# Attention's constants made ahead of batch 0's rows, and the feed-forward weights rounded in nine blocks of columns

## The chip, the cores and the metric

The kernel runs on one core of a Trainium2 chip. The metric is the device time of one launch in microseconds. The core's engines work side by side and meet at semaphores only: TensorE (PE in the profile: matmuls), the vector engine (DVE), ScalarE (ACT), GpSimd (POOL) and SyncE (SP, which here only issues DMAs). Each takes its instructions in the order in which the program wrote them for it.

## What is computed

A "macaron" block over x of shape (8, 512, 256): half a feed-forward layer, an attention layer, half a feed-forward layer again, each on a layer norm of its input.

```python
x = x + 0.5 * ffn(layernorm(x))
x = x + attn(layernorm(x))
x = x + 0.5 * ffn(layernorm(x))

def ffn(x):                      # gate_w, up_w: (256, 768), down_w: (768, 256)
    gate = silu(quantized_matmul(x, gate_w, gate_scale))
    up = quantized_matmul(x, up_w, up_scale)
    return quantized_matmul(gate * up, down_w, down_scale)

def quantized_matmul(x, w, scale):
    return (x @ w.astype(float8_e4m3fn).astype(float32)) * scale
```

Attention is a gated delta rule with 16 heads of 128 channels, its sequence cut into chunks of 128 rows; the kernel solves each chunk's triangular system by a blocked inverse of six levels. For that it needs constants: an identity in f32 and f16, a few masks, and for each level a mask (`masks`) and a copy of the identity's right halves (`y16`).

## The kernel before

Three programs run one behind the other: `ffn_phase(first=True)`, `attention_phase` and `ffn_phase(first=False)`. Each ends with a barrier of all engines. The change touches the first only, which takes up to about 235 us of the span.

**Start of the first phase.** SyncE issues the loads: batch 0 of x, `gate_w`, batch 1, `up_w`, `down_w`, small things, then the other batches and the first four parts of the attention's weights. The DVE computes the statistics of batch 0 (`stats(0, 0)`), GpSimd the root and shift of the norm (`root(0, 0)`), ScalarE applies them (`normed(0, 0)`), TensorE transposes, ScalarE writes the high half in f16 (`high`) and the DVE the low half (`low(0, 0)`). Meanwhile the DVE rounds the three weights to the values of float8 e4m3, in `wq16`: for each weight six instructions over 128 x 1536 columns (lines 521 to 528), each waiting for the one before. It counts in `s_wd`. Between the first and the second weight stand `low(0, 0)` and `stats(0, 1)`. Then come four small instructions on the weights of the decays (the fourth raises `s_wd` to 4), and `hidden(0, 0)`.

**Turns.** Batch b has 512 rows and six blocks m of 128 hidden columns. For each block TensorE makes `gate(b, m)` and `up(b, m)` (four matmuls over 512 columns each), ScalarE `silu(b, m)`, the DVE `hidden(b, m)` (the product), ScalarE `hidden_high(b, m)`, GpSimd `low(b, m)` (the low half, L332) and TensorE `down(b, m)`. There are three buffers for the hidden block, so `hidden(b, m)` waits for `low` of three blocks ago, over batches too: `need(dve, g_hl, q - HB + 1)` with q = 6b + m and HB = 3. After block 5 the DVE scales (`added`, L434) and GpSimd adds to the rows (`added`, L342). Then the norm for attention of that batch runs in the next turn: `stats(1, b - 1)`, `root(1, b - 1)`, `normed(1, b - 1)`, transposes, `high(1)`, `low(1)`; and its decays (`decay_products`, `decays`, `logistic`, `cumulative`, `strengths`), which are stored as rows.

The order of each engine within a turn is written out by hand in `turn1(b)`. For GpSimd it is `low(b,0)`, `root(1,b-1)`, `low(b,1)`, `low(b,2)`, `low(b,3)`, `root(0,b+2)`, `low(b,4)`, `low(b,5)`, `added(b)`. Between two turns it makes constants: `attention_constants()` after turn 0, and `level_constants(li)`, li = b - 1, after turns 1 to 6. Every instruction of these waits for the one before (`chain`).

For the DVE it is `hidden(b,1)`, `stats(1,b-1)`, `hidden(b,2)`, `part_low(b,0)`, `hidden(b,3)`, `logistic(b-2)`, `stats(0,b+2)`, `hidden(b,4)`, `cumulative(b-2)`, `strengths(b-2)`, `low(1,b-1)`, `hidden(b,5)`, `part_low(b,1)`, `low(0,b+1)`, `added(b)`, `part_low(b,2)`, `hidden(b+1,0)`.

**Parts.** From turn 1 on three of the 20 parts of attention's weights are split in a turn, `part_high` on ScalarE and `part_low` (L473) on the DVE. The first five stay in SBUF; from the sixth on SyncE stores them, and `part_high` waits until its slot of two has been stored. ScalarE's order in a turn ends with `part_high(b+1,1)`, `silu(b+1,2)`, `hidden_high(b+1,1)`, `silu(b+1,3)`, `hidden_high(b+1,2)`, `decays(b-1)`, `normed(1,b)`, and the next begins with `silu(b,4)`.

Of the kernel before, what the change touches and what calls it, by code (L numbers as in the profile page):

```python
# [9 lines left out]
I32 = mybir.dt.int32  # L10
# [5 lines left out]
FF = 768  # L16
# [44 lines left out]
def ffn_phase(nc, first, x_in, y_out, stream, z16, kit, scratch, w):  # L61

    with ExitStack() as ctx:  # L63
# [36 lines left out]
        if first:  # L100
            wraw = sb("wraw", [P, 3 * KT * FF]); wexp = sb("wexp", [P, KT * FF])
# [4 lines left out]
            heads0 = sb("heads0", [NH, NC, CX]); blocks = sb("blocks", [P, P])  # L106
            raw = sb("raw", [P, RAW, PART]); pairs = sb("pairs", [P, 2, 2, PART], F16)
# [52 lines left out]
        def _(sp):  # L160
# [60 lines left out]
            if first:  # L221
# [7 lines left out]
                for x in range(RAW):  # L229
                    load_part(x)  # L230
                sp.wait_ge(s_wd, 4)
                sp.dma_start(w_saved, wq16[:, :]).then_inc(s_save, 16)
# [20 lines left out]
        def _(pool):  # L253
# [42 lines left out]
            def level_constants(li):  # L296

                if not 0 <= li < NL:
                    return
                mb, y16 = LEVELS[li], kit["y16"]  # L300
                nb = P // (2 * mb)

                blk = blocks[:, :].rearrange("p (b two m) -> p b two m", two=2, m=mb)[:, :, 0, :]
                chain(nc.gpsimd.memset(blocks[:, :], 0.0))
                chain(nc.gpsimd.memset(blk, -1.0))
                fill(blk, 0.0, ALU.is_ge, -mb, [[-2 * mb, nb], [0, mb]], 1)
                fill(blk, 0.0, ALU.is_ge, 2 * mb - 1, [[2 * mb, nb], [0, mb]], -1)
                fill(blocks[:, :], -1.0, ALU.not_equal, 0, [[-1, P]], 1)
                chain(nc.gpsimd.tensor_copy(kit["masks"][:, li].rearrange("p (b m) -> p b m", m=mb), blk))
                for u in range(U):  # L310
                    chain(nc.gpsimd.tensor_copy(halves(y16[:, li, u], mb, 1), halves(kit["ident"][:, :], mb, 1)))

# [65 lines left out]
        @block.vector  # L378
        def _(dve):
# [88 lines left out]
            def part_low(b, k):  # L468
                x = part_of(b, k)
                if x is None:  # L470
# [4 lines left out]
                    .then_inc(d_part, 1)  # L475

            def attention_scales():

                dve.wait_ge(s_prm, 16 * 8)
                nc.vector.tensor_scalar(prm[:, :, :, 0:TAPS], prm[:, :, :, 0:TAPS], 1.0 / WS, None, ALU.mult)  # L480
                nc.vector.tensor_scalar(lnwn[:, :], lnwn[:, :], -1.0, None, ALU.mult)

            def turn1(b):
                hidden(b, 1)
                stats(1, b - 1)
                hidden(b, 2)
                part_low(b, 0)
                hidden(b, 3)
# [24 lines left out]
            if first:  # L513
                stats(0, 0)
                for i in range(3):
                    r, q = wraw[:, i * KT * FF:(i + 1) * KT * FF], wq16[:, i * KT * FF:(i + 1) * KT * FF]
                    e = wexp[:, :]
                    dve.wait_ge(s_w[i], 16)


                    chain(nc.vector.tensor_scalar(e.bitcast(I32), r.bitcast(I32), 0x7F800000, None, ALU.bitwise_and))
                    chain(nc.vector.tensor_scalar(e, e, 2.0 ** -6, 1.5 * 2.0 ** 20, ALU.max, ALU.mult))
                    chain(nc.vector.tensor_tensor(r, r, e, ALU.add))
                    chain(nc.vector.tensor_tensor(r, r, e, ALU.subtract))


                    chain(nc.vector.tensor_scalar(e, r, 1.125 * 2.0 ** 119, 0.0, ALU.mult, ALU.mult))
                    nc.vector.tensor_tensor(q, r, e, ALU.add).then_inc(s_wd, 1)
                    dve.wait_ge(s_wd, i + 1)
                    if i == 0:  # L530
                        low(0, 0)
                        stats(0, 1)
                dve.wait_ge(s_small, 16 * 7)
# [9 lines left out]
            if first:  # L543
                hidden(0, 0)
                for b in range(0, B + 2):
                    turn1(b)
                    if b == 5:
                        attention_scales()
            else:
                for b in range(-3, B + 1):  # L550
                    turn2(b)

        @block.scalar
        def _(act):
# [95 lines left out]
            if first:  # L650
                normed(0, 0)
                high(0, 0)
                normed(0, 1)
            act.wait_ge(s_small, 16 * (7 if first else 3))
            if first:
                act.wait_ge(s_const, 8)
            if first:
# [11 lines left out]
        def _(pe):  # L669
# [20 lines left out]
            def gate(b, m):  # L690
                if not 0 <= b < B:
                    return
                q = MT * b + m
                if m == 0:
                    if b == 0:
                        pe.wait_ge(*((s_wd, 1) if first else (s_w[0], 16)))
                    pe.wait_ge(a_zh[0], KT * (b + 1))
                    pe.wait_ge(d_zl[0], KT * (b + 1))
# [3 lines left out]
            def up(b, m):  # L702
                if not 0 <= b < B:
                    return
                if m == 0 and b == 0:
                    pe.wait_ge(*((s_wd, 2) if first else (s_w[1], 16)))
                need(pe, a_sg, MT * b + m)
# [11 lines left out]
            def down(b, m):  # L719
# [3 lines left out]
                q = MT * b + m  # L723
                pe.wait_ge(g_hl, q + 1)
                if m == 0:
                    if b == 0:
                        pe.wait_ge(*((s_wd, 4) if first else (s_w[2], 16)))
                    need(pe, d_y, KT * b)
# [974 lines left out]
```

## Time and profile before

| | us |
|---|---|
| median of 3 runs (2473.37 to 2475.38) | 2474.54 |
| the profiled execution, whole | 2475.66 |
| its span in the profile | 2473.9 |
| busy TensorE | 2355.2 (95%) |
| busy DVE | 2017.3 (82%) |
| busy ScalarE | 1813.7 (73%) |
| busy GpSimd | 1824.8 (74%) |

The profile is of one execution. Times in its timeline are microseconds from the span's start. A row gives the start, the time taken, the engine, the line, the operation, the tiles (out<-in, the program's names with buffer numbers left out) and the shape; `x4` means that four in a row were merged, and the time is then of all four. In brackets stands how long the engine sat idle before and what ended that; "issue" is time in which it waited for nothing that the profile shows.

### The profile page before, as it was taken

Reading aid. Unit: us, or ns where it says so; the run is one execution under the profiler, and the core shown is the slowest. Engines: PE = TensorE matmul, PEld = TensorE weight load, DVE = VectorE, ACT = ScalarE, POOL = GpSimd, SP = SyncE. Lnnn points to the kernel's source line nnn. Section 1 sums busy time; section 2 is a strip of 40 time slices with the busy share of each in tenths; the row PEclk is TensorE's granted clock in tenths of the full one; section 3 lists DMA queues with packets and bytes.
Section 4 is the critical chain, followed back from the end, with each engine's and each line's share of the span. In section 5 each row is a group of like instructions: output and inputs, shape, how many; then the busy total and the mean of one; then the engine's idle time right before and its main releaser. Section 6 shows DMA issues by size and latency. Waiting matters only on the chain. (4 is left out here: it accounts for less than half of the span.)

```text
span 2473.9 us, 64148 instructions
## 1 busy us (share of the span) xinstructions
PE 2355.2 (95%) x24496; PEld 1825.3 (74%) x24496; DVE 2017.3 (82%) x4246; ACT 1813.7 (73%) x3567; POOL 1824.8 (74%) x1977
## 2 busy tenths in 40 slices
PE   4897899999999999999999999999999999998598
PEld 2553588888888888888888888888888878877365
DVE  7775888888888888888888888888888888886353
ACT  3673677777777777777777777777777777776364
POOL 4783577777777777777777877777777787777365
PEclk9998999999999999999999999999999999999699
DMA  6241011111121111111211111112211111111001
GB/s 165 91 144 43 27 32 32 30 27 30 31 57 49 31 32 31 32 32 32 52 52 30 32 32 32 32 31 49 54 30 29 31 32 32 32 32 23 22 32 38
DMA packets 72833, 103.59 MB, mean 42 GB/s; under 512 B 21456, under 2 KB 33744, under 8 KB 72400
## 3 DMA queue, kind: packets, MB, share of 16 engines
q1 hardware_dynamic: 72528, 99.48, 15.9%
q8 instruction: 197, 3.23, 0.5%
q14 instruction: 108, 0.88, 0.1%
HBM read 85.69 MB, written 13.77 MB: 40 GB/s over the span
## 5 line engine op out<-in xcount | busy, mean ns | idle before, releaser
L1598 PE MATMUL a_bank<-k_z,k_kqv 128*128 128x512 f16 x2304 | 598.9, 380 | 9.8 <-DVE a_qb L1173 3.8
L1287 ACT ACTIVATE a_inv<-a_bank 128x512 f16<-128x512 f32 x640 | 383.3, 599 | 207.0 <-PE a_bank L1447 191.2
L1104 DVE TENSOR_TENSOR k_y<-a_bank,k_masks 128x256 f16<-128x256 f32 x768 | 318.8, 415 | 126.0 <-PE a_bank L1433 122.0
L941 POOL TENSOR_TENSOR k_diag<-k_ident,k_bcol 128x512 f32<-128x512 f32 x128 | 132.9, 1038 | 228.7 <-DVE a_prod L1080 213.7
L1598 PEld LDWEIGHTS a_bank<-k_z,k_kqv 128*128 128x128 f16 x2304 | 198.1, 98 | 139.7 <-DVE a_kb L1173 5.9
L1173 DVE SCALAR_TENSOR_TENSOR a_kb<-a_bank,k_prm,a_kb 128x511 f32<-128x511 f32 (+2 forms) x384 | 283.1, 737 | 14.9 <-ACT a_kb L1231 14.4
L1173 DVE SCALAR_TENSOR_TENSOR a_vb<-a_bank,k_prm,a_vb 128x511 f32<-128x511 f32 (+2 forms) x384 | 283.9, 739 | 0.1
L1173 DVE SCALAR_TENSOR_TENSOR a_qb<-a_bank,k_prm,a_qb 128x511 f32<-128x511 f32 (+2 forms) x384 | 282.8, 737 | 0.4
L1447 PE MATMUL a_bank<-a_inv,k_y 128*128 128x64 f16 x3072 | 271.4, 192 | 1.0 <-DVE k_y L1104 1.0
L1445 PE MATMUL a_bank<-k_y,a_inv 128*128 128x64 f16 x2560 | 236.0, 193 | 4.8 <-DVE k_y L1104 2.2
L1433 PEld LDWEIGHTS a_bank<-a_inv,a_am 128*128 128x128 f16 x3072 | 168.1, 98 | 94.4 <-ACT a_inv L1287 5.6
L1447 PEld LDWEIGHTS a_bank<-a_inv,k_y 128*128 128x128 f16 x3072 | 207.1, 98 | 34.2 <-DVE k_y L1104 1.3
L1445 PEld LDWEIGHTS a_bank<-k_y,a_inv 128*128 128x128 f16 x2560 | 197.1, 98 | 43.7 <-DVE k_y L1104 17.7
L953 POOL TENSOR_TENSOR a_am<-a_at,k_ident 128x512 f16<-128x512 f32 x128 | 163.7, 1279 | 82.0 <-DVE a_at L1089 82.0
L1029 POOL TENSOR_SCALAR a_gb<-a_gb 128x512 f32<-128x512 f32 x128 | 219.7, 1716 | 1.2 <-ACT a_gb L1251 1.2
L1433 PE MATMUL a_bank<-a_inv,a_am 128*128 128x64 f16 x3072 | 215.6, 193 | 4.3 <-ACT a_inv L1287 4.0
L1598 PE MATMUL a_bank<-k_z,k_gate 128*128 128x512 f16 x768 | 200.8, 379 | 0.2 <-DVE a_vb L1173 0.2
L1578 PE MATMUL a_bank<-k_wo,a_oh 128*128 128x256 f16 x1024 | 191.2, 275 | 9.6 <-POOL a_ol L1045 9.3
L1312 ACT ACTIVATE a_on<-a_bank,a_shift,a_rstd 128x128 f32<-128x128 f32 x512 | 191.7, 463 | 6.6 <-POOL a_shift L1021 6.5
L1540 PE MATMUL a_bank<-a_wv,a_mix 128*128 128x128 f32 x1024 | 185.6, 278 | 0.7 <-DVE a_wv L1123 0.7
L1080 DVE TENSOR_TENSOR_SCAN a_prod<-a_decay,k_diag 128x516 f32<-128x516 f32 x128 | 182.2, 1424 | 1.2 <-ACT a_kdec L1262 1.2
L1038 POOL TENSOR_TENSOR a_oa<-a_oa,a_gb 128x512 f32<-128x512 f32 x128 | 163.0, 1274 | 22.4 <-ACT a_oa L1321 21.7
(152 smaller groups left out, 6696.7 us busy)
## 6 DMA issues: line engine op xcount, KB each, us to landing
a_decay<-decay_rows SPq DMA_DIRECT2D x128, 258.0 KB, 3.8
a_cum<-cumulative_rows SPq DMA_DIRECT2D x96, 258.0 KB, 3.6
weight_pairs<-f_pairs SPq DMA_DIRECT2D x15, 512.0 KB, 2.9
k_kqv<-weight_pairs SPq DMA_DIRECT2D x9, 512.0 KB, 4.7
stream<-in_L_attn_x SPq DMA_DIRECT2D x8, 512.0 KB, 6.8
out<-stream SPq DMA_DIRECT2D x8, 512.0 KB, 2.9
f_raw<-in_L_attn_Wk SPq DMA_DIRECT2D x4, 512.0 KB, 4.8
f_raw<-in_L_attn_Wq SPq DMA_DIRECT2D x4, 512.0 KB, 5.0
```

Source lines behind the costliest of these rows:

```text
L1029: nc.gpsimd.tensor_scalar(gb[:, n % 2, j], gb[:, n % 2, j], 1.0, None, ALU.add).then_inc(m["pool_one"], 1)
L1080: nc.vector.tensor_tensor_scan(prod[:, :], decay[:, :], diag[:, :, :].rearrange("p u x -> p (u x)"), 0.0, ALU.mult, ALU.add).then_inc(m["d ...
L1104: nc.vector.tensor_tensor(even(y16[:, j], mb), bank[LEV[par]][:, 0:U * C // 2].rearrange("p (u b m) -> p u b m", u=U, m=mb), masks[:, j].r ...
L1173: nc.vector.scalar_tensor_tensor(out=dst[:, d:S], in0=bank[PJ[j % 2]][:, 0:S - d], scalar=prm[:, i, U * (n // B) + j, TAPS - 1 - d:TAPS - ...
L1287: nc.scalar.activation(both, bank[LEV[par]][:, :].rearrange("p (two b m) -> p two b m", two=2, m=mb), ACT.Copy).then_inc(m[f"act_lev{par}" ...
L1312: ins = nc.scalar.activation(on[:, u], bank[OUT][:, u * D:(u + 1) * D], ACT.Identity, bias=shift[:, u:u + 1], scale=rstd[:, u:u + 1])
L1433: mm = pe.matmul(at_half(LEV[par], 0, u), am16[:, par, u], halves(t16[par][:, u], mb, 0), start=True, stop=True)
L1445: pe.matmul(at_half(LEV[par], 0, u), tt16[par][:, u], halves(y16[:, j, u], mb, 0), start=True, stop=True)
L1447: mm = pe.matmul(at_half(LEV[par], half, u), y16[:, j, u], halves(tt16[par][:, u], mb, 1), start=True, stop=True)
L1540: mm = pe.matmul(units(OUT)[:, u], mix[:, t % 2, u], wv[:, u], start=not c, stop=True)
L1578: mm = pe.matmul(bank[SUM][:, 0:H], o[:, u], wo16[:, group % WO_SLOTS, wh, u], start=(u == 0 and wh == 0 and o is oh), stop=(u == U - 1 an ...
L1598: mm = pe.matmul(bank[PJ[j % 2]][:, :], wt, z16[:, zh, k, cols], start=(x == 0), stop=(x == 5))
```

## The change

Four things change, all in `ffn_phase(first=True)`.

1. The rounding goes by `quantise(i, x)`: a third of weight i, which is two of its six blocks of 128 hidden columns, so that each of the six instructions works on 128 x 512 columns. `wexp` is a third as large. `s_wd` now counts nine pieces, and ten with the small weights.
2. The DVE's order at the start becomes: (0,0), (1,0), (0,1), `low(0,0)`, (1,1), `hidden(0,0)`, (0,2), `hidden(0,1)`, `stats(0,1)`, (1,2), `hidden(0,2)`, (2,0), `hidden(0,3)`, (2,1), (2,2), the small weights, then turn 0 without its first `hidden`. On ScalarE `normed(0,1)` moves from ahead of `silu(0,0)` to behind `silu(0,3)`. TensorE waits in batch 0 for the piece that it needs, and `decay_products(0)` for `s_wd` = 10.
3. GpSimd makes all constants ahead of turn 0: `root(0,0)`, `attention_constants()`, `level_constants(0)`, `root(0,1)`, `level_constants(1..5)`, `turn1(0)`, and nothing between the turns.
4. `level_constants` builds its mask in place in f16, by a memset and three fills over 64 columns, in place of two memsets, three fills and a cast by way of `blocks`; its four copies read the identity in f16.

```diff
+ROUNDED = ((1, 3, 5), (2, 4, 6), (7, 8, 9))
...
-                sp.wait_ge(s_wd, 4)
+                sp.wait_ge(s_wd, 9)
                 sp.dma_start(w_saved, wq16[:, :]).then_inc(s_save, 16)
...
+                mask = kit["masks"][:, li].rearrange("p (b m) -> p b m", m=mb)
+                chain(nc.gpsimd.memset(mask, -1.0))
+                fill(mask, 0.0, ALU.is_ge, -mb, [[-2 * mb, nb], [0, mb]], 1)
+                fill(mask, 0.0, ALU.is_ge, 2 * mb - 1, [[2 * mb, nb], [0, mb]], -1)
+                fill(mask, -1.0, ALU.not_equal, 0, [[-2 * mb, nb], [-1, mb]], 1)
+                for u in range(U):
+                    chain(nc.gpsimd.tensor_copy(halves(kit["y16"][:, li, u], mb, 1),
+                                                halves(kit["ident16"][:, :], mb, 1)))
...
             if first:
                 root(0, 0)
+                attention_constants()
+                level_constants(0)
                 root(0, 1)
+                for li in range(1, NL):
+                    level_constants(li)
                 for b in range(0, B + 2):
                     turn1(b)
-                    if b == 0:
-                        attention_constants()
-                    level_constants(b - 1)
...
+            def quantise(i, x):
+
+                if x == 0:
+                    dve.wait_ge(s_w[i], 16)
+                r, q = third(wraw, i, x), third(wq16, i, x)
+                e = wexp[:, :].rearrange("p (k n) -> p k n", n=r.shape[2])
...
+                chain(nc.vector.tensor_scalar(e.bitcast(I32), r.bitcast(I32), 0x7F800000, None, ALU.bitwise_and))
+                chain(nc.vector.tensor_scalar(e, e, 2.0 ** -6, 1.5 * 2.0 ** 20, ALU.max, ALU.mult))
+                chain(nc.vector.tensor_tensor(r, r, e, ALU.add))
+                chain(nc.vector.tensor_tensor(r, r, e, ALU.subtract))
...
+                chain(nc.vector.tensor_scalar(e, r, 1.125 * 2.0 ** 119, 0.0, ALU.mult, ALU.mult))
+                nc.vector.tensor_tensor(q, r, e, ALU.add).then_inc(s_wd, 1)
+                dve.wait_ge(s_wd, ROUNDED[i][x])
...
                 stats(0, 0)
...
+                quantise(0, 0)
+                quantise(1, 0)
+                quantise(0, 1)
+                low(0, 0)
+                quantise(1, 1)
+                hidden(0, 0)
+                quantise(0, 2)
+                hidden(0, 1)
+                stats(0, 1)
+                quantise(1, 2)
+                hidden(0, 2)
+                quantise(2, 0)
+                hidden(0, 3)
+                quantise(2, 1)
+                quantise(2, 2)
```

## Rows read from the trace of the kernel before

**Rows 1.** Windows, 100 to 200 us: busy us by engine (instructions), granted clock, DMA share.
```profile
100.00:200.00 100.00, 90.84 (x540) 51.48 (x538) 77.10 (x144) 69.01 (x116) 80.16 (x113) 1.00 0.42 130
```

**Rows 2.** Timeline of the DVE, 7 to 46 us.
```profile
7.03 0.96 DVE L521 TENSOR_SCALAR f_wexp<-f_wraw 128x1536 int32<-128x1536 int32 x1 [0.15 <-DMA f_wraw<-in_L_ffn_gate_w]
...
9.03 1.76 DVE L523 TENSOR_TENSOR f_wraw<-f_wraw,f_wexp 128x1536 f32<-128x1536 f32 x1
...
37.01 1.41 DVE L423 SCALAR_TENSOR_TENSOR f_hid<-f_bank,f_us,f_sg 128x512 f32<-128x512 f32 x2
...
45.41 0.75 DVE L423 SCALAR_TENSOR_TENSOR f_hid<-f_bank,f_us,f_sg 128x512 f32<-128x512 f32 x1
```

**Rows 3.** Timeline of GpSimd, 9 to 62 us.
```profile
9.95 0.89 POOL L324 TENSOR_TENSOR f_shift<-f_nmean,f_rstd 128x4 f32<-128x4 f32 x1
...
55.58 0.20 POOL L282 MEMSET k_ident<- 128x128 f32 x1
...
57.23 2.66 POOL L286 MEMSET k_y<- 128x3072 f16 x1
...
61.67 1.15 POOL L332 TENSOR_TENSOR f_hl<-f_hid,f_hh 128x512 f16<-128x512 f32 x1
```

**Rows 4.** Groups by line and form, 0 to 225 us: xcount | busy us, mean ns | idle before.
```profile
L542 DVE TENSOR_SCALAR f_hds<-f_hds 128x256 f32<-128x256 f32 x1 | 0.3, 289 | 0.0
...
L537 DVE TENSOR_TENSOR f_wabl<-f_wab,f_wabh 128x64 f16<-128x64 f32 x1 | 0.2, 226 | 0.0
```

**Rows 5.** SyncE's timeline; then DMA issues by tile: KB, us from issue to landing.
```profile
2.35 0.55 SPq L205 DMA_DIRECT2D f_wraw<-in_L_ffn_up_w  x1
...
f_wraw<-in_L_ffn_up_w SPq DMA_DIRECT2D x1, 768.0 KB, 8.1
```

**Rows 6.** Timeline of GpSimd, 128 to 132 us: one level's fills, copies, and the next `low`.
```profile
128.15 1.08 POOL L276 TENSOR_SCALAR_AFFINE_SELECT f_blocks<-f_blocks 128x64 f32<-128x64 f32 x3
...
129.60 1.13 POOL L311 CAST k_y<-k_ident 128x64 f16<-128x64 f32 x4
130.82 1.16 POOL L332 TENSOR_TENSOR f_hl<-f_hid,f_hh 128x512 f16<-128x512 f32 x1
```

**Rows 7.** Timeline of all engines, 152 to 161 us: batch 5's turn.
```profile
152.94 1.06 ACT L608 ACTIVATE f_pairs<-f_raw 128x1024 f16<-128x1024 f32 x1 [1.49 <-DMA weight_pairs<-f_pairs]
...
154.47 0.62 ACT L590 ACTIVATE f_hh<-f_hid 128x512 f16<-128x512 f32 x1
...
155.33 1.25 DVE L473 SCALAR_TENSOR_TENSOR f_pairs<-f_raw,f_pairs 128x1024 f16<-128x1024 f32 x1
...
156.08 0.66 ACT L598 ACTIVATE f_ab<-f_bank,f_bab 32x512 f32<-32x512 f32 x1
...
157.93 2.07 ACT L561 ACTIVATE f_ztok<-stream,f_shift,f_rstd 128x256 f32<-128x256 f32 x4 [1.19 <-POOL f_shift L324]
...
160.66 0.75 DVE L423 SCALAR_TENSOR_TENSOR f_hid<-f_bank,f_us,f_sg 128x512 f32<-128x512 f32 x1 [1.36 <-issue]
```

**Rows 8.** Timeline of all engines, 77 to 84 us: `part_low`, and a level's copies beside it.
```profile
77.67 1.92 DVE L473 SCALAR_TENSOR_TENSOR k_kqv<-f_raw,k_kqv 128x1024 f16<-128x1024 f32 x1
...
82.91 1.59 POOL L311 CAST k_y<-k_ident 128x64 f16<-128x64 f32 x2
```

**Rows 9.** Timelines of DVE and ScalarE: end of `stats(1,0)`, `hidden(1,4)`, `hidden(2,4)`, `normed(1,6)`.
```profile
58.01 0.38 DVE L402 BATCH_NORM_AGGREGATE f_mv<-f_bn 128x2 f32<-128x6 f32 x4
...
67.29 0.75 DVE L423 SCALAR_TENSOR_TENSOR f_hid<-f_bank,f_us,f_sg 128x512 f32<-128x512 f32 x1 [1.86 <-ACT f_sg L581]
...
90.79 0.75 DVE L423 SCALAR_TENSOR_TENSOR f_hid<-f_bank,f_us,f_sg 128x512 f32<-128x512 f32 x1 [1.53 <-ACT f_sg L581]
...
202.98 2.08 ACT L561 ACTIVATE f_ztok<-stream,f_shift,f_rstd 128x256 f32<-128x256 f32 x4 [1.46 <-POOL f_shift L324]
```

**Rows 10.** Timeline of TensorE, 69 to 72 us: pairs of matmuls at either clock.
```profile
69.10 1.06 PE L714 MATMUL f_bank<-f_zh,f_wq 128*128 128x512 f16 x2
...
71.46 0.59 PE L714 MATMUL f_bank<-f_zl,f_wq 128*128 128x512 f16 x2
```

More of the change, by code:

```diff
@@ L100, in ffn_phase @@
         if first:
-            wraw = sb("wraw", [P, 3 * KT * FF]); wexp = sb("wexp", [P, KT * FF])
+            wraw = sb("wraw", [P, 3 * KT * FF]); wexp = sb("wexp", [P, KT * FF // 3])
             wab = sb("wab", [P, KT, 2 * NH]); wab64 = sb("wab64", [P, KT, 2 * NH])
@@ L105, in ffn_phase @@
             ab = sb("ab", [2 * NH, 2, NC, CX]); gx = sb("gx", [NH, 2, NC, CX])
-            heads0 = sb("heads0", [NH, NC, CX]); blocks = sb("blocks", [P, P])
+            heads0 = sb("heads0", [NH, NC, CX])
             raw = sb("raw", [P, RAW, PART]); pairs = sb("pairs", [P, 2, 2, PART], F16)
@@ L151, in part_of, with third @@
             return x if 0 <= x < PARTS else None
+        def third(ap, i, x):
+            part = ap[:, i * KT * FF:(i + 1) * KT * FF]
+            if i < 2:
+                return part.rearrange("p (k n) -> p k n", k=KT)[:, :, 2 * x * P:2 * (x + 1) * P]
+            return part.rearrange("p (m n) -> p m n", m=MT)[:, 2 * x:2 * (x + 1)]
         def rows_stored(pairs):
@@ L296, in level_constants @@
             def level_constants(li):
-                if not 0 <= li < NL:
-                    return
-                mb, y16 = LEVELS[li], kit["y16"]
+                mb = LEVELS[li]
                 nb = P // (2 * mb)
[L303 to L309, printed above, removed]
+                mask = kit["masks"][:, li].rearrange("p (b m) -> p b m", m=mb)
[3 more added lines that the diff above has]
+                fill(mask, -1.0, ALU.not_equal, 0, [[-2 * mb, nb], [-1, mb]], 1)
                 for u in range(U):
-                    chain(nc.gpsimd.tensor_copy(halves(y16[:, li, u], mb, 1), halves(kit["ident"][:, :], mb, 1)))
+                    chain(nc.gpsimd.tensor_copy(halves(kit["y16"][:, li, u], mb, 1),
+                                                halves(kit["ident16"][:, :], mb, 1)))
             def root(n, e):
@@ L483, in turn1 @@
             def turn1(b):
-                hidden(b, 1)
+                if b:
+                    hidden(b, 1)
                 stats(1, b - 1)
-                hidden(b, 2)
+                if b:
+                    hidden(b, 2)
                 part_low(b, 0)
-                hidden(b, 3)
+                if b:
+                    hidden(b, 3)
                 logistic(b - 2)
@@ L514, in _ @@
                 stats(0, 0)
[L515 to L532, printed above, removed]
+                quantise(0, 0)
[13 more added lines that the diff above has]
+                quantise(2, 2)
                 dve.wait_ge(s_small, 16 * 7)
@@ L543, in _ @@
             if first:
-                hidden(0, 0)
                 for b in range(0, B + 2):
@@ L652, in _ @@
                 high(0, 0)
-                normed(0, 1)
             act.wait_ge(s_small, 16 * (7 if first else 3))
@@ L663, in _ @@
                 silu(0, 3)
+                normed(0, 1)
                 hidden_high(0, 2)
@@ L693, in gate @@
                 q = MT * b + m
+                if b == 0 and first:
+                    pe.wait_ge(s_wd, ROUNDED[0][m // 2])
+                elif b == 0 and m == 0:
+                    pe.wait_ge(s_w[0], 16)
                 if m == 0:
-                    if b == 0:
-                        pe.wait_ge(*((s_wd, 1) if first else (s_w[0], 16)))
                     pe.wait_ge(a_zh[0], KT * (b + 1))
@@ L704, in up @@
                     return
-                if m == 0 and b == 0:
-                    pe.wait_ge(*((s_wd, 2) if first else (s_w[1], 16)))
+                if b == 0 and first:
+                    pe.wait_ge(s_wd, ROUNDED[1][m // 2])
+                elif b == 0 and m == 0:
+                    pe.wait_ge(s_w[1], 16)
                 need(pe, a_sg, MT * b + m)
@@ L724, in down @@
                 pe.wait_ge(g_hl, q + 1)
+                if b == 0 and first:
+                    pe.wait_ge(s_wd, ROUNDED[2][m // 2])
+                elif b == 0 and m == 0:
+                    pe.wait_ge(s_w[2], 16)
                 if m == 0:
-                    if b == 0:
-                        pe.wait_ge(*((s_wd, 4) if first else (s_w[2], 16)))
                     need(pe, d_y, KT * b)
@@ L740, in decay_products @@
                     return
+                if e == 0:
+                    pe.wait_ge(s_wd, 10)
                 pe.wait_ge(a_zh[1], KT * (e + 1))
```

## Prediction

> **What bounds the kernel now.** The chain of waits reaches back over 5% of the span only, so the bound has to be read by stage. I read first the busy time by stretch, then the timelines of the engines over the first stage (0 to 221 us), the only one that the diff touches; everything later starts behind that stage's closing barrier, so a shift of its end should pass through one to one. In the stretch 100 to 200 TensorE is busy 90.8% of the time and nobody else over 81% [rows 1], yet it isn't alone on the path. In batch 5's turn, and alike in those beside it, the DVE's `hidden(b,4)` waits for ScalarE's `normed(1,b-1)`, which waits for GpSimd's `root(1,b-1)`, and that stands behind `level_constants` [rows 7]. Before 37 us the path is the DVE: three rounded blocks, each six chained instructions over 1536 columns, and `hidden(0,0)` only behind all three [rows 2].
>
> **The rounding in nine pieces.** A `tensor_scalar` takes 0.289 us for 256 columns and 0.96 for 1536, a `tensor_tensor` 0.226 for 64 and 1.76 for 1536 [rows 2, 4]. By straight lines 512 columns take 0.43 and 0.69. A piece is 3 x 0.43 + 3 x 0.69 + 6 x 0.035 (the gap of chained instructions) = 3.56 us; nine make 32.0 where three blocks made 25.1: +7.0 us of DVE work. The second weight lands at 2.35 + 8.1 = 10.45 us [rows 5], as the second piece wants it (7.03 + 3.56 = 10.6): no wait. TensorE's new waits have only matmuls of the same batch behind them, and those need the piece anyway. SyncE waits for the ninth piece before it stores the weights; behind it are two small loads and `save_part`, which wants nothing before turn 1. I cost both at nothing; the cover is a DVE that is later than they are.
>
> **GpSimd's order, the heart of it.** Its new queue is `root(0,0)`, attention constants, level 0, `root(0,1)`, levels 1 to 5, and only then `low(0,0)`. But `hidden(0,3)` needs `low(0,0)` (three buffers), and behind `hidden(0,3)` in the DVE's queue stand the pieces (2,1) and (2,2), `stats(0,2)` and `hidden(0,4)`. And `root(0,1)` waits for `stats(0,1)`, which now stands behind five pieces. So five levels run after that, with batch 0 waiting. Costs: the attention constants take 61.67 - 55.58 = 6.1 us, 2.66 of it one memset [rows 3]. A level in its new form is a memset (0.15), three fills (1.08 in one group before; about 1.0) and four copies (1.13) with gaps: 2.45 us alone [rows 6].
>
> They don't run alone. Where a DVE instruction with two SBUF inputs meets GpSimd's reads, one stands still: `part_low` took 1.92 beside GpSimd's `added`, 1.25 otherwise; two copies took 1.59 beside `part_low`, where four take 1.13; the four-column `f_shift` took 0.89 beside the rounding [rows 3, 6 to 8]. So beside the rounding about one reading GpSimd instruction passes for each DVE instruction, and costs the DVE some 0.1 us. Memsets beside a `tensor_tensor` pass; beside a `tensor_scalar` no row shows it. Bounds for the 2.66 us memset: it costs the DVE 0 to 2.7; I take 1.3, the middle, since three of six instructions in a piece are of that kind. Apart from this sum: the Trainium skill, "SBUF — State Buffer", Who interferes with whom, states that a DVE instruction in a 2-port mode, which `tensor_scalar` can enter, and any GpSimd instruction exclude each other, whoever issued first; by it the memset would cost up to the 1.7 us that remain when the next `tensor_scalar` comes, in place of 1.3.
>
> The walk: 7.03 + 5 pieces 17.8 + `low(0,0)` 1.3 + two `hidden` 1.45 + `stats(0,1)` 1.8 + interference (11 x 0.1 + 1.3) = 31.7. `root(0,1)` 2.3, ends near 34. By 39.5 the DVE has done the rest of piece (1,2), `hidden(0,2)` and piece (2,0), while 10 of GpSimd's 35 reads passed. The other 3.75 levels run alone, 9.2 us: 48.7. `low(0,0)` 1.16 [rows 6]: `hidden(0,3)` starts at 49.9. Then the DVE: 0.75, two pieces 7.1, of which `low(0,1..3)` (1.16 each, reading) block some 2.3, small ones 1.1, `stats(0,2)` 1.8: `hidden(0,4)` at 63.0 where it was 45.41 [rows 2]: **+17.6**. TensorE sat nearly idle meanwhile and runs its next matmuls at the lower level (1.2 GHz; a pair over 512 columns took 1.06 where it takes 0.59 at 2.4 GHz), [rows 10]; on the few that nothing hides there, three to four, that is +0.7: **+18.3** at the start of turn 1.
>
> **What is won back.** Turn 1: the 6.1 us of constants go from GpSimd. `stats(1,0)` ended at 58.4, so `root(1,0)` (pow about 1.0, its last step held by `part_low`) would end at 60.2, `normed(1,0)` (2.07) at 62.3, `hidden(1,4)` at 63.0 rather than 67.29 [rows 9]: 4.3; TensorE's clock doesn't fall after the gap that this leaves now (the pairs of 1.06 at 69.1, back to 0.59 at 71.5, [rows 10]), 1.3 more: -5.6. Turn 2, level 0 gone, no store waits yet: `normed(1,1)` follows `decays`, `hidden(2,4)` at 87.9 rather than 90.79 [rows 9]: -2.8. Turns 3 to 5, from P = 152.94, where ScalarE's `part_high(b,1)` gets its slot back [rows 7]: ScalarE alone would reach `normed` at P + 3.8, the end of `decays`, rather than P + 5.0, a gain of 1.2. But GpSimd is free now and starts `low(b,1)` at P + 2.2, when `hidden_high(b,1)` ends, just ahead of the DVE's `part_low` at P + 2.4 [rows 7]. That reads SBUF twice and is held about 1.0, `logistic` behind it once more by `low(b,2)`; then `stats(0,b+2)` 1.8, and `hidden(b,4)` comes at P + 7.8, where it is now (160.66 = P + 7.7). I take 0 for each of the three, with 1.2 as the other end. Turns 6 and 7 have no `stats(0,b+2)`: -1.0 and -1.2 (`normed(1,6)` waited 1.46 for the root, [rows 9]). Sum: -10.6, up to -14.9.
>
> **The sum.** 18.3 - 10.6 = +7.7 on the profiled span of 2473.9, whose run took 2475.66. The median of the three runs is 2474.54, 1.1 lower; the difference is put on the median: 2482.2 us.
>
> **Rivals.**
> *Mild interference, within 0.2%.* If the locks cost less (the memset nothing, the three `low` nothing) the start loses 14.0, and the DVE wins the port in turns 3 to 5, giving 12.9: +1.1, at 2475.6. For it: the gaps of 0.035 are short, and who wins a port is a matter of 0.2 us. Against: 0.89 for a four-column instruction. What lies between this and the forecast is part of the case. 27%.
> *The levels hide (faster).* One mechanism: GpSimd's short instructions run at full pace beside the rounding. Then `stats(0,1)` ends at 29.3, the root at 31, five levels at 43.3, `hidden(0,3)` at 44.5, `hidden(0,4)` at 55.3: +9.9 - 14.9 = -5.0, 2469.5. It decides from the point where the startup loses less than the 14.9 that the turns can give back. The two copies of 1.59 speak against it [rows 8]. 8%.
> *The pieces lose the double pace.* The `tensor_scalar` over two strips of 256 columns may run at one column a cycle: 0.69 for 0.43. On the path lie 5 pieces ahead of `stats(0,1)` and 2 behind `hidden(0,3)`: 21 x 0.26 = +5.5, 2487.7. No row has such a strip; the strips are long and contiguous. 8%.
> *The change doesn't do what it says.* The rows of batch 0 do go between the pieces in both queues; only `hidden(0,3)` and later don't gain. This is the forecast itself.
>
> **Chances.** Forecast 57%: 2482.2, own range 2478 to 2487. The rivals as above. A measurement of this kernel can tell about 0.2%, 5 us, from no change. The forecast's low end and the first rival lie within that: slower 0.61, same 0.31, faster 0.08. Range 2473.5 to 2488: it leaves out the faster rival and the far end of the slow one.
>
> **What would show it.** Right: in the timeline of the DVE `hidden(0,3)` follows an idle time of about 10 us that GpSimd's `f_hl` ends, near 50 us; `f_bn` of batch 2 near 61; nine groups of rounding with `tensor_tensor` near 0.69; level constants in one row between 34 and 49, 2.45 each towards the end. `hidden(1,4)` 14.0 us later than now (18.3 - 4.3); turns 3 to 5 still 23.2 apart, 6 and 7 shorter. Wrong: the wait is missing (GpSimd's queue does not matter), levels of 2.4 us beside the rounding (no interference), turns 3 to 5 at 22 (the port isn't lost to `low(b,1)`), or an end of the first stage that moves while the end of the kernel doesn't.

## The result, and the profile after

The changed kernel takes 2480.33 us (median of 18 runs, 2477.59 to 2481.52); the kernel before took 2474.82 in the runs beside it (18 runs, 2471.04 to 2475.99). The ratio is 1.0021, with a 95% interval of 1.0015 to 1.0027: 5.5 us, 0.2% slower. Forecast were +7.7 and 2482.2. The profiled execution's span is 2479.7 where before's was 2473.9, so +5.8.

The first stage can be followed by one instruction per batch, `hidden(b,4)` on the DVE, and by the first instruction behind the stage's closing barrier, GpSimd's first `k_diag`. What remains of the span behind that is the third figure. From the DVE's and GpSimd's timelines, in us:

| | before | after | shift | forecast |
|---|---|---|---|---|
| `hidden(0,4)` | 45.4 | 61.5 | +16.1 | +17.6 |
| `hidden(1,4)` | 67.3 | 80.9 | +13.6 | +14.0 |
| `hidden(2,4)` | 90.8 | 100.8 | +10.0 | +9.9 (18.3 - 5.6 - 2.8) |
| `hidden(3,4)` | 114.2 | 122.9 | +8.7 | +9.9 |
| `hidden(4,4)` | 137.5 | 144.6 | +7.1 | +9.9 |
| `hidden(5,4)` | 160.7 | 167.0 | +6.3 | +9.9 |
| `hidden(7,4)` | 205.7 | 209.8 | +4.1 | +7.7 |
| first `k_diag` | 236.5 | 240.7 | +4.2 | +7.7 |
| the span behind it | 2237.4 | 2239.0 | +1.6 | 0 |

So the start cost about what was forecast, turns 1, 2, 6 and 7 gave back about what was forecast, turns 3 to 5 gave back 3.7 where I had put nothing, and 1.6 came on top behind the stage.

The wait that the forecast hangs on is there. GpSimd's timeline of the changed kernel, 30 to 52 us (start, duration, engine, line, operation, out<-in; in brackets the idle time before it and what ended it). `root(0,1)` has the lines 323 to 328, a level's memset, fills and copies have 309, 284 and 314, `low` has 336:

```profile
30.81 0.22 POOL L323 TENSOR_TENSOR f_var<-f_mv,f_epsd 128x4 f32<-128x4 f32 x1 [10.99 <-issue]
...
34.88 2.35 POOL L314 COPY k_y<-k_ident 128x64 f16<-128x64 f16 x4
...
44.19 1.13 POOL L314 COPY k_y<-k_ident 128x64 f16<-128x64 f16 x4
...
47.80 3.56 POOL L336 TENSOR_TENSOR f_hl<-f_hid,f_hh 128x512 f16<-128x512 f32 x3
```

GpSimd stood idle for 10.99 us until `stats(0,1)` came from the DVE, and only then did `root(0,1)` and the five levels run, one behind the other, with `low(0,0)` last. The DVE's timeline, 30 to 62 us:

```profile
30.28 0.38 DVE L407 BATCH_NORM_AGGREGATE f_mv<-f_bn 128x2 f32<-128x6 f32 x4
...
37.63 0.69 DVE L497 TENSOR_TENSOR f_wq<-f_wraw,f_wexp 128x512 f16<-128x512 f32 x1
49.09 0.75 DVE L428 SCALAR_TENSOR_TENSOR f_hid<-f_bank,f_us,f_sg 128x512 f32<-128x512 f32 x1 [10.77 <-POOL f_hl L336]
49.76 0.60 DVE L490 TENSOR_SCALAR f_wexp<-f_wraw 128x512 int32<-128x512 int32 x1
50.39 1.26 DVE L491 TENSOR_SCALAR f_wexp<-f_wexp 128x512 f32<-128x512 f32 x1
...
52.41 1.52 DVE L493 TENSOR_TENSOR f_wraw<-f_wraw,f_wexp 128x512 f32<-128x512 f32 x1
...
61.55 0.72 DVE L428 SCALAR_TENSOR_TENSOR f_hid<-f_bank,f_us,f_sg 128x512 f32<-128x512 f32 x1
```

The DVE, the engine that was the path before [rows 2], stands still for 10.77 us ahead of `hidden(0,3)`, released by GpSimd's `low`. Between that and `hidden(0,4)` it still has 12.5 us of its own work, two pieces of rounding among it, so batch 0 is late by 16.1. In the stretch 100 to 200 us the stage is denser than before: TensorE is busy 93.1% of it, where it was 90.8% [rows 1].

```profile
100.00:200.00 100.00, 93.13 (x590) 57.60 (x590) 83.74 (x148) 74.19 (x123) 69.55 (x69) 1.00 0.42 130
```

### The profile page after: what moved, and what is told of

The parts are those of the page before. It is cut to its first block and busy times, and to the rows that moved or that the text cites. A ratio compares the mean times of both kernels' runs of the same rounds, so it can differ in the third digit from the quotient of the medians.

```text
span 2479.7 us, 64188 instructions
## 1 busy us (share of the span) xinstructions
PE 2355.9 (95%) x24496; PEld 1827.5 (74%) x24496; DVE 2030.7 (82%) x4282; ACT 1815.7 (73%) x3567; POOL 1820.7 (73%) x1965
## 5 line engine op out<-in xcount | busy, mean ns | idle before, releaser
L1475 PEld LDWEIGHTS a_bank<-k_y,a_inv 128*128 128x128 f16 x2560 | 197.0, 98 | 43.6 <-DVE k_y L1134 17.6
L1068 POOL TENSOR_TENSOR a_oa<-a_oa,a_gb 128x512 f32<-128x512 f32 x128 | 163.1, 1274 | 22.4 <-ACT a_oa L1351 21.7
```

The lines of the kernel that those rows point to most:

```text
L1475: pe.matmul(at_half(LEV[par], 0, u), tt16[par][:, u], halves(y16[:, j, u], mb, 0), start=True, stop=True)
```

## The experiments

The theory: GpSimd's queue at the start costs (five levels between `root(0,1)` and `low(0,0)`), the shorter turns pay, and nine pieces cost 7 us of DVE work whatever the order. The rivals: the rounding alone makes the kernel late and the queue is harmless; or the turns gain from the rounding's order rather than from GpSimd's. In each experiment all of the computation is done. In all of them the kernel before took 2474.65 (30 runs beside experiments 1 to 4) or 2474.55 (15 runs beside 5 to 8).

**1. The changed kernel with levels 1 to 5 behind the last turn.**

```diff
                 root(0, 1)
-                for li in range(1, NL):
-                    level_constants(li)
                 for b in range(0, B + 2):
                     turn1(b)
+                for li in range(1, NL):
+                    level_constants(li)
```

> The changed kernel with levels 1 to 5 made by GpSimd behind its last turn, where it is idle for 14 us (from 221.5 to 235 in the trace of the changed kernel), in place of ahead of turn 0. Theory (GpSimd's queue is the loss: hidden(0,3) waits 10.8 us for low(0,0) behind five levels): the wait is gone, hidden(0,3) starts near 40 instead of 49.1, hidden(0,4) near 51.7 instead of 61.55, and the time is 9.5 lower than the changed kernel's, about 2471. Rival (the 7 us more of rounding on the DVE is the whole loss, the wait only hides it): hidden(0,4) stays within 3 us of 61.55, time 2478 or more.

Measured: 2472.16 (2469.56 to 2472.82), 0.9988 of before (0.9979 to 0.9996). `hidden(0,3)` starts at 41.1 in place of 49.1, `hidden(0,4)` at 52.5 in place of 61.5, the stage ends at 231.8. Moving five levels, and nothing else, turned the loss into a small gain: their place in the queue is what costs.

**2. The nine pieces alone, GpSimd's constants in their old form and place.** Against the changed kernel:

```diff
                 root(0, 0)
-                attention_constants()
-                level_constants(0)
                 root(0, 1)
-                for li in range(1, NL):
-                    level_constants(li)
                 for b in range(0, B + 2):
                     turn1(b)
+                    if b == 0:
+                        attention_constants()
+                    level_constants(b - 1)
```

> The changed kernel's rounding in nine pieces with its order on DVE, ScalarE and TensorE, but GpSimd's constants in their old form and places between the turns. Theory: no long wait of hidden(0,3); the pieces cost the DVE 7 us, of which the overlap with batch 0 gives some back: hidden(0,4) near 50.4 instead of 45.41 in the kernel before, the turns behind unchanged, so 5 us slower than before: 2479.8. Rival (the overlap pays for the pieces, all of the loss is GpSimd's): within 1 us of before, 2474.8.

Measured: 2479.2 (2478.42 to 2482.15), 1.002 of before (1.0011 to 1.0028). `hidden(0,4)` comes at 51.1, 5.7 late, and the stage's end 5.5 late, at 241.97: the turns take what they took before. So the pieces alone lose some 5 us and win nothing back, and the turns' gain belongs to GpSimd's part.

**3. GpSimd's part alone, on the kernel before.** The converse of experiment 2, on the whole blocks:

```diff
                 root(0, 0)
+                attention_constants()
+                level_constants(0)
                 root(0, 1)
+                for li in range(1, NL):
+                    level_constants(li)
                 for b in range(0, B + 2):
                     turn1(b)
-                    if b == 0:
-                        attention_constants()
-                    level_constants(b - 1)
```

> The kernel before with GpSimd's part of the change alone (constants ahead of turn 0, masks made in place), rounding in three blocks. Theory: five levels still stand ahead of low(0,0), which ends near 49; hidden(0,3) waits about 6 us, hidden(0,4) at 51.7 instead of 45.41; the turns then give back the same 11.9 us as in the changed kernel: 5.6 us faster than before, 2469. Rival (the turns' gain was only the catching up of a late start, bound by something that a late start hides): no faster than before, 2474 or more.

Measured: 2470.8 (2464.94 to 2474.01), 0.9984 (0.9975 to 0.9993). The DVE's timeline:

```profile
37.00 1.41 DVE L420 SCALAR_TENSOR_TENSOR f_hid<-f_bank,f_us,f_sg 128x512 f32<-128x512 f32 x2
...
48.55 0.75 DVE L420 SCALAR_TENSOR_TENSOR f_hid<-f_bank,f_us,f_sg 128x512 f32<-128x512 f32 x1 [6.56 <-POOL f_hl L328]
...
52.10 0.75 DVE L420 SCALAR_TENSOR_TENSOR f_hid<-f_bank,f_us,f_sg 128x512 f32<-128x512 f32 x1 [1.08 <-PE f_bank L711]
```

`hidden(0,0)` starts at 37.00 as before (37.01, [rows 2]), though attention's constants, level 0 and most of level 1 ran beside the rounding. The rounding was 0.3 ahead of before's at 12.3 us, so their reads cost the DVE 0.3 in all. The same wait for `low` stands ahead of `hidden(0,3)`, but here no piece of rounding is behind it, and batch 0 loses 6.7 where it loses 16.1 with both parts. The two parts are worth +4.6 and -3.9 apart, +0.7 in sum, and +5.5 together. `hidden(0,3)` comes as late here (48.55) as in the changed kernel (49.09), though `stats(0,1)` ends 11.7 us earlier: beside whole blocks GpSimd is slower. From its timeline in experiment 3, level 0's copies, the start of `root(0,1)` and level 1's fills:

```profile
21.42 6.11 POOL L306 COPY k_y<-k_ident 128x64 f16<-128x64 f16 x4
27.61 0.87 POOL L315 TENSOR_TENSOR f_var<-f_mv,f_epsd 128x4 f32<-128x4 f32 x1
...
31.46 4.63 POOL L276 TENSOR_SCALAR_AFFINE_SELECT k_masks<-k_masks 128x64 f16<-128x64 f16 x3
```

So the levels delay `hidden(0,3)`, with or without the pieces, and what the two parts do together is what stands behind it: 12.5 us up to `hidden(0,4)` with the pieces, 3.6 here. The pieces alone (experiment 2) have the long stretch too, but there `hidden(0,3)` starts at 39.6.

**4. Whole blocks, attention's constants at the front, all six levels behind the last turn.** Against before, with the levels in their new form:

```diff
                 root(0, 1)
+                attention_constants()
                 for b in range(0, B + 2):
                     turn1(b)
-                    if b == 0:
-                        attention_constants()
-                    level_constants(b - 1)
+                for li in range(0, NL):
+                    level_constants(li)
```

> The kernel before (three blocks), attention's constants behind root(0,1), where GpSimd is idle from 23 to 38.5, and all six levels in the new form behind the last turn. Theory: nothing is added to the start but 1 us (the 2.66 us memset against a tensor_scalar), hidden(0,4) near 46.5; the turns give 11.9: 2464 to 2465, faster than both kernels. The six levels take 14.7 us where GpSimd is idle for about 15: at most 1 us of them shows. Rival (the stage is held by TensorE and the DVE, constants matter little): 2470 or more.

Measured: 2467.29 (2465.29 to 2470.5), 0.9971 (0.9961 to 0.9982), some 3 us above what I expected. Two things ate that. GpSimd's memset now met a `tensor_scalar` of the rounding, and the last levels ended just ahead of the barrier. From the timelines of the DVE and of GpSimd:

```profile
27.36 2.44 DVE L517 TENSOR_SCALAR f_wexp<-f_wraw 128x1536 int32<-128x1536 int32 x1
```

```profile
26.33 2.66 POOL L286 MEMSET k_y<- 128x3072 f16 x1
...
227.47 1.14 POOL L306 COPY k_y<-k_ident 128x64 f16<-128x64 f16 x4
229.12 1.04 POOL L937 TENSOR_TENSOR k_diag<-k_ident,k_bcol 128x512 f32<-128x512 f32 x1 [0.51 <-POOLq L63]
```

The `tensor_scalar` took 2.44 where the same takes 0.96 [rows 2], so the memset held it 1.48. The first `k_diag` follows the last level after 0.51 idle, where GpSimd had been idle for 15 us at this place in the kernel before: six levels at the very end had become the path.

**5. Levels 1 to 5 each written twice** (the same values again), which prices the queue by doubling it:

```diff
                 for li in range(1, NL):
                     level_constants(li)
+                    level_constants(li)
```

> The changed kernel with each of levels 1 to 5 made twice ahead of low(0,0) (the second time writes the same values). Theory: the five levels lie on the path of batch 0 with their full time, 2.41 us each as in its trace from 40.5 on: hidden(0,3) starts 12.1 later than 49.1 and the time is 12.1 above the changed kernel's 2480.3: 2492.4. Rival (the turns or the closing barrier take up a late start): 2486 or less.

Measured: 2491.98 (2491.14 to 2492.91, 4 runs), 1.007 (1.0057 to 1.0084). `hidden(0,3)`, in the DVE's timeline:

```profile
61.63 0.75 DVE L429 SCALAR_TENSOR_TENSOR f_hid<-f_bank,f_us,f_sg 128x512 f32<-128x512 f32 x1 [23.32 <-POOL f_hl L336]
```

It starts 12.5 later than the changed kernel's at 49.09: five levels of 2.45, and 0.3. The kernel is 11.7 longer than the changed one. So a microsecond of work between `root(0,1)` and `low(0,0)` costs nearly a microsecond of the kernel.

**6. `root(0,1)` behind all six levels.** If `root(0,1)` doesn't stand ahead of the levels, they needn't wait for `stats(0,1)`:

```diff
                 attention_constants()
-                level_constants(0)
-                root(0, 1)
-                for li in range(1, NL):
+                for li in range(NL):
                     level_constants(li)
+                root(0, 1)
```

> The changed kernel with all six levels ahead of root(0,1), so that levels 1 to 5 fill the 11 us from 19.8 in which GpSimd waits for stats(0,1). Theory (the order on one queue is what costs): beside the rounding a level takes about 4 us, so they end near 39 and low(0,0) near 42; hidden(0,3) starts near 42.1 instead of 49.1, 7 us less: 2473.3. Rival (interference slows levels and rounding so far that nothing is won): 2478 or more.

Measured: 2473.6 (2472.37 to 2474.75), 0.9996 of before (0.9987 to 1.0004). `hidden(0,3)` starts at 41.65, 7.4 earlier than in the changed kernel, by moving one call, and the kernel is 6.7 shorter. The idle 10.99 of GpSimd ahead of `root(0,1)` was room for three of the five levels; the other two ran on to 38.6. The copies of a level took 1.1 to 2.5 beside the pieces rather than 1.13. So the loss against before goes with the order of one call. The work of the pieces still costs: experiment 7, with whole blocks, is 7.6 lower than this one.

**7. Whole blocks, the constants and two levels at the front, four behind the last turn.** What experiments 3 and 4 point to:

```diff
                 root(0, 0)
+                attention_constants()
+                level_constants(0)
                 root(0, 1)
+                level_constants(1)
                 for b in range(0, B + 2):
                     turn1(b)
-                    if b == 0:
-                        attention_constants()
-                    level_constants(b - 1)
+                for li in range(2, NL):
+                    level_constants(li)
```

> The kernel before (three rounded blocks) with attention's constants and level 0 ahead of root(0,1), level 1 behind it, and levels 2 to 5 behind the last turn. Theory: in the run with the constants alone these first ones ended at 37.4, ahead of hidden(0,0)'s low half, and the DVE's hidden(0,0) stayed at 37.0, so the start costs nothing; four levels (9.7 us) fit under the closing chain, where six held the barrier by 2.3 us. 1.5 + 2.3 less than with all levels last: 2463.5. Rival (the last levels never held the barrier): 2465.8.

Measured: 2466.0 (2464.69 to 2467.07, 5 runs), 0.9965 (0.9951 to 0.9978): faster than both kernels. From GpSimd's timeline:

```profile
218.76 1.13 POOL L306 COPY k_y<-k_ident 128x64 f16<-128x64 f16 x4
225.18 1.04 POOL L939 TENSOR_TENSOR k_diag<-k_ident,k_bcol 128x512 f32<-128x512 f32 x1 [5.29 <-POOLq L63]
```

GpSimd waits 5.29 us for the barrier, and `hidden(0,0)` starts at 37.10: neither end is held by constants any more. The stage ends at 225.2, 3.9 before experiment 4's, as expected; but the span behind it is 2239.1 in place of 2236.6, so the time falls by 1.3 only.

**8. As 7, with `part_low` ahead of `hidden(b,2)`,** to take the DVE's `part_low` out of the way of GpSimd's `low`, the contention on which my zero for turns 3 to 5 rested. Against experiment 7:

```diff
                 stats(1, b - 1)
-                hidden(b, 2)
                 part_low(b, 0)
+                hidden(b, 2)
                 hidden(b, 3)
```

> The kernel of e7 with the DVE's part_low(b,0) ahead of hidden(b,2) instead of behind it. Theory (in the turns GpSimd's low(b,1) holds part_low(b,0) by about 0.9 us, and it stands on the DVE's way to hidden(b,4)): it then fills the 1.4 to 1.8 us in which the DVE waits for silu(b,2), free of low(b,1); hidden(b,4) comes about 1 us earlier in turns 3 to 5, 3 to 5 us in all: about 2460. Rival (ScalarE's chain through the store of the parts sets the turns): same as e7 within 1 us.

Measured: 2464.61 (2464.17 to 2467.77, 5 runs), 0.9962 (0.9949 to 0.9974). The DVE's timelines, first of experiment 7, then of experiment 8:

```profile
101.18 2.08 DVE L471 SCALAR_TENSOR_TENSOR f_pairs<-f_raw,f_pairs 128x1024 f16<-128x1024 f32 x1
```

```profile
99.68 1.19 DVE L471 SCALAR_TENSOR_TENSOR f_pairs<-f_raw,f_pairs 128x1024 f16<-128x1024 f32 x1
...
103.61 1.35 DVE L443 TENSOR_SCALAR f_ab<-f_ab 32x512 f32<-32x512 f32 x1 [0.25 <-ACT f_ab L596]
```

In turn 3 `part_low` is free of the lock (1.19 for 2.08), but `logistic` takes it over (1.35). In turns 4 and 5 there was nothing to free: `part_low(b,0)` took 1.22 in experiment 7 too, so my expectation of 0.9 in each of three turns was wrong there. From `hidden(2,4)` to `hidden(3,4)` the turn is 0.3 shorter (21.72 for 22.03), the three turns together are not (67.58 for 67.56). That is the rival, the same within 1 us; whether the store sets the turns, as it says, comes below. The stage ends at 226.29, 1.1 later than in experiment 7, for a reason that has nothing to do with the move: `hidden(0,4)` is already 1.2 late (46.85 for 45.66), ahead of the first `part_low`. TensorE's timelines, first of experiment 7, then of experiment 8:

```profile
40.44 0.85 PE L712 MATMUL f_bank<-f_zl,f_wq 128*128 128x512 f16 x2
```

```profile
42.11 1.06 PE L712 MATMUL f_bank<-f_zl,f_wq 128*128 128x512 f16 x2
```

In that execution of experiment 8 the pairs still take 1.06, the time of the lower level [rows 10], up to 42.96, where in experiment 7 they are back at 0.59 from 41.1 on, with the same instructions ahead. The 1.4 by which the median fell comes from behind the stage (2236.6 in place of 2239.1).

## Why the prediction was right, and where it wasn't

**The order and its wait: right.** The step "five levels run after that, with batch 0 waiting" is the 10.77 us idle time ahead of `hidden(0,3)`, which starts at 49.1 (forecast 49.9). Experiments 1, 5 and 6 show the cause from three sides.

**The pieces: right.** 0.43 and 0.69 for the two kinds of instruction held, so the rival of the lost double pace (0.69 for a `tensor_scalar`) is out. Experiment 2 has the price of the pieces alone, 5.5 at the stage's end, for 7.0 of added DVE work.

**The memset: right in kind, 0.96 for my 1.3.** The DVE's and GpSimd's timelines of the changed kernel:

```profile
10.85 0.71 DVE L491 TENSOR_SCALAR f_wexp<-f_wexp 128x512 f32<-128x512 f32 x1
11.59 0.69 DVE L492 TENSOR_TENSOR f_wraw<-f_wraw,f_wexp 128x512 f32<-128x512 f32 x1
...
13.04 1.39 DVE L496 TENSOR_SCALAR f_wexp<-f_wraw 128x512 f32<-128x512 f32 x1
```

```profile
10.56 0.72 POOL L293 MEMSET k_diag<- 128x516 f32 x1
11.33 2.82 POOL L294 MEMSET k_y<- 128x3072 f16 x1
```

The `tensor_scalar` that began inside the memset of `k_y` took 1.39 for 0.43 and ended just behind it; the one beside the smaller memset of `k_diag` lost 0.28, which I had not priced. The `tensor_tensor` beside the same memset took its usual 0.69, and in experiment 3 one took its usual 1.76. The Trainium skill, "SBUF — State Buffer", Who interferes with whom, which the prediction weighed against my 1.3, has it that such a `tensor_scalar` and a GpSimd instruction exclude each other, and that the one issued first keeps the port to its end. The traces agree: 1.11 us of the memset were left here and 1.63 in experiment 4, and the instruction lost 0.96 and 1.48.

**Short reads beside the rounding: too dear.** I put 0.1 on the DVE for each; experiment 3 shows 0.3 for all of them together. In the changed kernel `stats(0,1)` ended at 30.66, not 31.7 (0.2 of that because the first weight landed 0.2 earlier), and the start was 16.1, not 17.6. That about one GpSimd read passes for each DVE instruction held: a level's four copies took 6.11 us beside blocks of 1536 columns (experiment 3), 2.35 beside pieces of 512, and 1.13 alone. The locks of the three `low` behind `hidden(0,3)` came to 1.83 (0.60, 1.26 and 1.52 where 0.43, 0.43 and 0.69 are usual; forecast 2.3).

**Turns 1 and 2: right by their ends** (+13.6 and +10.0 for +14.0 and +9.9), as were turns 6 and 7 together (2.2 for 2.2). From `hidden(0,4)` on, though, turns 1 and 2 gave back 6.2 where the forecast had 7.7.

**The clock: a second fall not foreseen.** I put +0.7 on TensorE's lower level behind the long wait, and 1.3 back because the clock would not fall in turn 1 any more. The pairs of 1.06 behind the wait are there, up to 53. But then TensorE was idle for 6.44, and ran at the lower level (1.2 GHz) once more, up to 70. From its timeline, and the window from 64 to 68 with its granted clock of 0.50:

```profile
64.60 0.39 PE L760 MATMUL f_bank<-f_wq,f_hh 128*128 128x256 f16 x1 [6.44 <-POOL f_hl L336]
...
68.84 1.06 PE L740 MATMUL f_bank<-f_zl,f_wq 128*128 128x512 f16 x2
...
70.40 0.59 PE L740 MATMUL f_bank<-f_zl,f_wq 128*128 128x512 f16 x2
```

```profile
64.00:68.00 4.00, 3.40 (x17) 2.24 (x18) 1.64 (x3) 3.62 (x7) 1.70 (x2) 0.50 0.02 4
```

In the gap of 1.55 at 78.8 the clock stayed at 1.00, as forecast. How much of the 1.5 that turns 1 and 2 fell short the second fall explains, no run shows.

**Turns 3 to 5: the step that failed.** I wrote "I take 0 for each of the three, with 1.2 as the other end". They gave 1.3, 1.6 and 0.8, together 3.7: the other end. My reason for the zero was that GpSimd's `low(b,1)` comes just ahead of the DVE's `part_low(b,0)`, holds it, and so keeps `hidden(b,4)` at P + 7.8. ScalarE's P, GpSimd and the DVE in the turns of batches 3 and 4 ("turn 3" and "turn 4" below):

```profile
115.44 1.06 ACT L630 ACTIVATE f_pairs<-f_raw 128x1024 f16<-128x1024 f32 x1 [1.76 <-DMA weight_pairs<-f_pairs]
...
117.67 3.26 POOL L336 TENSOR_TENSOR f_hl<-f_hid,f_hh 128x512 f16<-128x512 f32 x2 [0.46 <-ACT f_hh L612]
117.83 2.08 DVE L478 SCALAR_TENSOR_TENSOR f_pairs<-f_raw,f_pairs 128x1024 f16<-128x1024 f32 x1
...
122.86 0.72 DVE L428 SCALAR_TENSOR_TENSOR f_hid<-f_bank,f_us,f_sg 128x512 f32<-128x512 f32 x1
...
136.70 1.06 ACT L630 ACTIVATE f_pairs<-f_raw 128x1024 f16<-128x1024 f32 x1
...
139.15 2.13 POOL L326 TENSOR_TENSOR f_rstd<-f_var,f_nhalf 128x4 f32<-128x4 f32 x1
139.19 1.22 DVE L478 SCALAR_TENSOR_TENSOR f_pairs<-f_raw,f_pairs 128x1024 f16<-128x1024 f32 x1
```

In turn 3 `low` does hold `part_low` (2.08 where 1.25 was usual, [rows 7]). In turns 4 and 5 it doesn't: `part_low` takes 1.22, and it is GpSimd's `root(1,b-1)` that is held (2.13 for 1.02), because it waited for `stats(1,b-1)`. So "the port isn't lost to `low(b,1)`", one of my own signs of being wrong, came true in two turns of three, and the turns took 22.1, 21.7 and 22.4. The first half of a turn kept its length all the same: `hidden(b,4)` comes 7.42, 7.89 and 7.92 behind P, before 7.97, 7.81 and 7.72.

What I left out is the rest of the turn, from `hidden(b,4)` to the next P: 13.84, 14.48 and 14.50, where it was 15.45, 15.47 and 15.39. `root(0,b+2)` stands there in GpSimd's queue. In batch 3's turn, first before, then changed:

```profile
118.27 1.85 POOL L324 TENSOR_TENSOR f_shift<-f_nmean,f_rstd 128x4 f32<-128x4 f32 x1
...
118.85 1.20 DVE L473 SCALAR_TENSOR_TENSOR f_pairs<-f_raw,f_pairs 128x1024 f16<-128x1024 f32 x1
...
123.48 1.29 DVE L434 TENSOR_TENSOR f_scaled<-f_bank,f_hds 128x512 f32<-128x512 f32 x2 [1.56 <-PE f_bank L732]
```

```profile
126.02 0.20 POOL L328 TENSOR_TENSOR f_shift<-f_nmean,f_rstd 128x4 f32<-128x4 f32 x1
...
126.67 1.74 DVE L478 SCALAR_TENSOR_TENSOR f_pairs<-f_raw,f_pairs 128x1024 f16<-128x1024 f32 x1
...
130.57 1.29 DVE L439 TENSOR_TENSOR f_scaled<-f_bank,f_hds 128x512 f32<-128x512 f32 x2 [0.42 <-PE f_bank L760]
```

Before, the root's last step (four columns) stands still until the DVE's `part_low(b,1)` is over, and with it `low(b,4)`, `low(b,5)`, the `down` of the batch and `added`, at `hidden(b,4)` + 9.27. In the changed kernel GpSimd gets there first: the step takes 0.20, and `added` comes at + 7.71, 8.35 and 8.35. The next P follows `added` by 6.1 to 6.2 in both kernels, through `part_low(b,2)` and the store of its part. So the store ends the turn, as it did, and it is `added` that comes earlier. In the turns of batches 3 to 5 this divides the ten kernels in two: with constants between the turns (before and experiment 2) the step takes 1.84 to 1.85 and `added` comes at + 9.27; in the eight others it takes 0.20 and `added` comes at + 7.7 to 8.9. No run moved the step by itself.

**Behind the stage: not foreseen.** I wrote that a shift of the stage's end "should pass through one to one". It passed through with 1.6 on top, 28% of the span's +5.8. The last section has what is known of it.

**The forecast as a whole.** On the span, step by step: up to `hidden(2,4)` +10.0 for +9.9, though by two errors that cancel (the start 1.5 too dear, turns 1 and 2 together 1.5 too generous); turns 3 to 5 -3.7 for 0; turns 6 and 7 -2.2 for -2.2; to the barrier +0.1; behind it +1.6 for 0. That makes 5.8 for 7.7, so a forecast within 2 us of the time had a term in it that was wrong by 3.7, nearly half covered by one that nobody had asked about: that part is luck. Two slips in the working: 10 of 35 reads leave 3.6 levels, not 3.75 (0.4 us), and the terms of the turns add up to 14.2 at most, not 14.9. Of the rivals, "the levels hide" failed at its first step: beside the rounding a level's copies took 2.35, not 1.13, and since GpSimd waited for `stats(0,1)` anyway, the pace decided little. Mild interference was right about turns 4 and 5, where the DVE won the port, and nearly right about what the turns give back (12.0 for 12.9); it was wrong about the start, which it put at 14.0.

## What to carry to other kernels

Work that "fills idle time" at the start of an in-order queue costs nothing only if everything ahead of it in that queue is ready early, and if its own pace beside its neighbours leaves the room (beside whole blocks a level's copies took 6.11 us in place of 1.13). In the changed kernel one call placed in front (`root(0,1)`, which waits for another engine) turned 11 us of free room into a stall, and moving it gave 6.7 us back. Two edits on one queue don't add up: +4.6 and -3.9 made +5.5, since one set its work behind an instruction that the other made wait. And when a turn is costed, it is followed round to its own beginning; an unchanged first half says nothing about the second.

## What the runs showed of the hardware

**The stage behind the change has two lengths.** The span behind the first `k_diag`, by profile, in us: 2237.4 before, 2239.0 after, 2239.2, 2237.6, 2239.1, 2236.6, 2237.1, 2237.1, 2239.1 and 2236.6 in experiments 1 to 8. The long ones (after, 1, 3, 7) are those in which TensorE's granted clock falls early in attention. Windows of the changed kernel (from:to, length, then busy us and instructions of TensorE, its weight loads, DVE, ScalarE, GpSimd; granted clock; DMA share):

```profile
262.00:270.00 8.00, 6.09 (x46) 3.55 (x44) 7.35 (x12) 3.53 (x6) 3.55 (x3) 1.00 0.05 18
270.00:278.00 8.00, 5.99 (x43) 3.18 (x44) 6.16 (x10) 4.75 (x11) 2.05 (x2) 0.81 0.19 66
276.00:279.00 3.00, 2.78 (x11) 1.04 (x9) 1.53 (x3) 0.69 (x2) 1.93 (x2) 0.59 0.16 54
```

and of the kernel before in the same stretches of its program, 4.2 us earlier:

```profile
257.80:265.80 8.00, 6.20 (x46) 3.60 (x44) 7.35 (x12) 3.43 (x6) 3.56 (x3) 1.00 0.07 21
265.80:273.80 8.00, 5.37 (x56) 3.06 (x56) 7.03 (x12) 5.73 (x13) 2.37 (x3) 1.00 0.25 66
```

Two rows of TensorE's timeline in the changed kernel, six matmuls of one form each:

```profile
275.97 2.69 PE L1628 MATMUL a_bank<-k_z,k_gate 128*128 128x512 f16 x6
...
279.95 1.47 PE L1628 MATMUL a_bank<-k_z,k_gate 128*128 128x512 f16 x6 [0.25 <-DVE a_vb L1203]
```

The first group ran at the lower of the two levels (1.2 GHz), 1.2 us longer than the second at 2.4 GHz; TensorE had been busy for 6.09 of the 8 us from 262, with gaps just ahead of the fall. Before, the first of the two stretches was the same (6.20 of 8) and the clock stayed at 1.00. Experiments 4 and 7 run the same attention code after first stages that differ in order alone, and one has the fall and the other hasn't. The price can be read closer: from the first `k_diag` to the fifth it is 63.6 us in the four executions with the fall and 61.8 to 62.0 in the six without, and the difference stays to the last (2014.4 to 2014.5, and 2012.5 to 2013.0). So the fall costs 1.4 to 2.0 us. What is left of the spread, about 1 us in experiments 4 and 8, lies behind the last `k_diag`. That the change causes the fall I can't say; no experiment moved it on purpose.

**A memset holds a `tensor_scalar` and not a `tensor_tensor`**: 1.39 for 0.43 and 2.44 for 0.96, against the usual 0.69 and 1.76. **Short GpSimd reads are slowed by a chained DVE, and hardly slow it**: a level's copies took two to five times as long, while the whole rounding lost 0.3. **A DVE scan over 16 x 516 isn't safe from GpSimd**: 2.08 beside its instructions in the turns of batches 2 to 5 of the kernel before; in the changed one 1.21 in batch 3's turn, 1.86 and 1.85 in the next two.
